# Cross attention: the last context row's values of all 16 heads as two products of 512 columns

## The chip, the cores and the metric

The kernel runs on one core of a Trainium2 chip. The metric is the device time of one execution in microseconds, the median over the runs. The profile is of one execution, with its own time.

## The reference

A block of three layers on x (64 batch items, 32 tokens, 512 channels), each added to its input: cross attention to a context of 257 rows of 256 channels per item, self attention with rotary positions, and a mixture of eight experts of which each token takes two. Only cross attention bears on the change:

```
Q  = (layernorm(x) @ Wq.T)           16 heads of 32
KV = ctx @ Wkv.T                     K and V, 16 heads of 32 each
A  = softmax(Q K^T * 32**-0.5)       over 257 context rows
x  = x + (A V) @ Wo.T
```

All is float32. The kernel makes most large products out of three float32r products each: an operand is split in a high part (rounded to float32r) and a low part (the rest), and high x high, low x high and high x low are added.

## The kernel before

**Tiling.** The 2048 queries are 16 tiles of 128, each four batch items (steps j = 0 to 3, s = 4 i + j) of 32 queries. K and V are never made: `absorb_k` (L353) multiplies the queries with Wk, so that `scores` (L373) works on the context itself, and `gather_z` (L385) makes U, the context summed with the attention weights, which `values` (L397) turns into heads with WvT. The context has 257 rows; 256 make two blocks of 128. The last row has its own way.

**The last row.** In the scores it is a column 256 of zT, filled by POOL (`last_key`, L648). For the values, setup multiplies the last rows of all 64 items with WvT on PE (L234), ACT copies the result to `vl` (L243), and SP stores it in DRAM (L207). For each tile, `last_values` on SP (L305) loads four blocks of 4 rows x 128 columns (512 bytes a row) into `VL` (16 rows x 512, block diagonal: row (m, j) has the values of item j for the four heads of group m in columns m). The weight of the last row is written by DVE to `p_last` (L627), 4 columns a step, at the point where it scales the exponentials; `turn_last` (L369) transposes it on PE into 16 rows in `bank_o`, and `last_rows` on DVE (L586) spreads it with `quad_mask` into `PL`, which is zero except where the row's item is the column's item. `values` then adds, for each of the 16 heads, one product of 16 rows (K) x 32 x 128 columns in full float32 to the two products with WvT:

```
for part in range(KL + 1):          # KL = 2; the third is the last row
    for hh in range(4):             # four column tiles of 32
```

Each float32 product is two records on PE in the profile. The four `hh` are on four column tiles of the array (`tile_position=(0, hh * HD)`).

**Order of the work.** Every engine has its order written out by hand; waits are on semaphores. The loop is by pairs of tiles, the first and last pair apart. PE in step j of tile i: `scores(s)`; at j = 0 `turn_last(i-1)`; `gather_z(s-1)`; at j = 2 `turn_x(i+2)`; `turn_z(s+1)`; `absorb_k`; at j = 0 `values(i-1)`, at j = 1 `project_o(i-1)`, at j = 2 and 3 half of `project_q(i+2)`; `turn_p(s)`. After the loop: `turn_last`, `gather_z`, `values`, `project_o` of the last tile. `scores` writes banks 0 to 3 of `bank_s`, of which 2 and 3 hold the transposed weights of the step before: its third and fourth blocks wait for `v_PT` (L379).

DVE in step j: two `nmax` (L616); at j = 0 `last_rows(i-1)`; at j = 1 `normalise`; reciprocal, `p_last`, scaling of Pr (L628); `qk_lo`, `z_lo`; at j = 0 `statistics` of tile i+2 (L141 to L146; not in the last two tiles) and `ot_lo(i-1)` (L594); `pt_lo` (L580); at j = 1 `add_residual`. ACT: four exp; at j = 0 `u_out`; `qk_hi`; at j = 2 `x_out`; otherwise `u_out`; `qk_out`; `z_hi`; at j = 0 `ot_hi` (L512); `pt_hi`; halves of `q_out`. SP: the four loads of z of a tile, each when its buffer is free, then `last_values`, which waits for `values` of the tile before; in the first tile also the weights of self attention (`ahead`) behind it. POOL: `last_key`, then `split_z` for `gather_z`, and `rstd_of`.

**Before the loop.** `block_constants` (L66) makes the identity and `quad_mask` on POOL in a block of its own, at whose end all engines meet. The setup block loads and transposes the weights; it too ends when all engines, SP's store of `vl` included, have come to its end.

## Time and profile before

| | us |
|---|---|
| median of 3 runs | 1562.9 |
| lowest, highest | 1562.47, 1563.0 |
| the profiled execution, its own time | 1564.86 |
| its span in the trace | 1563.1 |
| PE busy in the span | 1473.5 (94%) |
| DVE, ACT, POOL busy | 1050.5, 828.1, 538.3 |

Busy times are of the whole span; cross attention is its first 726 us, which the loop of tiles fills from about 50 us on. PE is TensorE's products, PEld its weight loads, which overlap them; DVE is VectorE, ACT ScalarE, POOL GpSimd, SP the engine that issues the loads. In a timeline, a row is an instruction or a run of like ones (x4): start and length in us, and in brackets how long the engine had idled before and what released it. Products overlap, so the time one costs is the distance between starts, not its length. PEclk is the granted clock of TensorE as a share of 2.4 GHz.

### The profile page before, as it was taken

To read this page: it belongs to the slowest core of one execution; us is meant where nothing else is said; L and a number is where in the kernel's file an instruction comes from. 1 tells how busy PE (TensorE), PEld (TensorE's weight loads), DVE (VectorE), ACT (ScalarE), POOL (GpSimd) and SP (SyncE) were. 2 spreads that over 40 slices of the span, in tenths; PEclk is the share of its full clock that TensorE was granted. 3 is DMA by queue.
4 is the path that set the end of the run, shared out by engine and by line. 5 is a ranking of instruction groups with operands and counts; after the bars stand their busy time and mean duration, and the time that the engine had idled before them with its cause. 6 is when DMAs were issued, how large, how long until landed. Compare 5 with 4: busy or idle time off the path is not lost. (4 is left out here: it accounts for less than half of the span.)

```text
span 1563.1 us, 40198 instructions
## 1 busy us (share of the span) xinstructions
PE 1473.5 (94%) x15376; PEld 1291.6 (83%) x15376; DVE 1050.5 (67%) x1832; ACT 828.1 (53%) x1542; POOL 538.3 (34%) x821
## 2 busy tenths in 40 slices
PE   5899999999999999997899998679999999999997
PEld 4788888888888888875687777579999999999996
DVE  1566666666666666663557676687878878787884
ACT  3566666666666666653434343154554545555552
POOL 1121222222222222221866777433333332333232
PEclk9999999999999999998999999789999999999999
DMA  8101000000000000000011014147887778787871
GB/s 291 50 22 29 29 23 26 27 20 27 27 27 21 26 27 27 22 15 1 16 37 36 32 41 150 57 150 248 272 273 269 262 245 291 248 265 247 292 240 41
DMA packets 127070, 173.85 MB, mean 111 GB/s; under 512 B 13097, under 2 KB 85737, under 8 KB 126962
## 3 DMA queue, kind: packets, MB, share of 16 engines
q1 hardware_dynamic: 116578, 145.29, 28.5%
q0 software_dynamic: 10384, 27.05, 4.8%
q8 instruction: 76, 1.25, 0.3%
q14 instruction: 32, 0.26, 0.1%
HBM read 157.05 MB, written 18.93 MB: 113 GB/s over the span
## 5 line engine op out<-in xcount | busy, mean ns | idle before, releaser
L1996 DVE TENSOR_TENSOR lo<-raw,hi 128x1024 fp32r<-128x1024 f32 x207 | 246.0, 1219 | 8.7 <-ACT hi L1932 7.4
L52 PE MATMUL mo_bank<-xT_hi,hi 128*128 128x256 f32 x768 | 217.3, 283 | 3.8 <-DVE xT_lo L2005 2.8
L54 PE MATMUL mo_bank<-xT_lo,hi 128*128 128x256 f32 x768 | 216.0, 281 | 0.0
L53 PE MATMUL mo_bank<-xT_hi,lo 128*128 128x256 f32 x768 | 216.0, 281 | 0.0
L1932 ACT CAST hi<-raw 128x1024 fp32r<-128x1024 f32 x207 | 208.3, 1048 | 5.6 <-PEq L842 2.8
L541 ACT ACTIVATE Pr<-xa_s,nmax 128x257 f32<-128x257 f32 x256 | 118.9, 471 | 122.9 <-DVE nmax L616 122.9
L1952 ACT ACTIVATE sl<-mo_bank 128x256 f32<-128x256 f32 x117 | 44.9, 384 | 251.2 <-PE mo_bank L54 251.2
L52 PEld LDWEIGHTS mo_bank<-xT_hi,hi 128*128 128x128 f32 x768 | 145.8, 190 | 10.7 <-issue 6.2
L52 PE MATMUL xa_s<-zT_hi,QK_hi 128*128 128x258 f32 x512 | 150.4, 294 | 2.9 <-DVE zT_lo L570 1.6
L53 PEld LDWEIGHTS mo_bank<-xT_hi,lo 128*128 128x128 f32 x768 | 145.5, 190 | 3.3
L54 PEld LDWEIGHTS mo_bank<-xT_lo,hi 128*128 128x128 f32 x768 | 145.8, 190 | 0.0
L53 PE MATMUL xa_s<-zT_hi,QK_lo 128*128 128x258 f32 x512 | 144.2, 282 | 0.0
L54 PE MATMUL xa_s<-zT_lo,QK_hi 128*128 128x258 f32 x512 | 143.9, 281 | 0.0
L2080 POOL TENSOR_TENSOR e_carrier<-count 128x1 f32<-128x1 f32 x84 | 25.4, 302 | 322.6 <-DMA of_row<-slot_val 114.2
L616 DVE TENSOR_REDUCE nmax<-xa_s 128x2 f32<-128x514 f32 x128 | 88.6, 692 | 47.9 <-PE xa_s L54 47.8
L583 DVE TENSOR_TENSOR PT_lo<-xa_s,PT_hi 128x512 fp32r<-128x512 f32 x128 | 82.3, 684 | 46.5 <-ACT PT_hi L510 46.2
L657 POOL TENSOR_TENSOR xa_carrier<-mhalf 128x1 f32<-128x1 f32 x64 | 12.6, 197 | 289.9 <-DVE QK_lo L575 285.3
L52 PE MATMUL xa_u<-PT_hi,zn_hi 128*128 128x512 f32 x256 | 103.4, 404 | 1.5 <-POOL zn_lo L660 1.5
L53 PE MATMUL xa_u<-PT_hi,zn_lo 128*128 128x512 f32 x256 | 101.5, 397 | 0.0
L54 PE MATMUL xa_u<-PT_lo,zn_hi 128*128 128x512 f32 x256 | 101.3, 396 | 0.0
L52 PE MATMUL mo_bank<-hi,a_hi 128*128 128x512 f32 x234 | 95.9, 410 | 5.2 <-DVE a_lo L2061 5.1
L52 PEld LDWEIGHTS xa_s<-zT_hi,QK_hi 128*128 128x128 f32 x512 | 96.4, 188 | 4.6 <-DVE zT_lo L570 3.0
(290 smaller groups left out, 3921.3 us busy)
## 6 DMA issues: line engine op xcount, KB each, us to landing
raw<-in_L_ffn_W_dram SPq DMA_DIRECT2D x207, 512.0 KB, 5.8
raw<-in_ctx_dram SPq DMA_DIRECT2D x64, 256.0 KB, 2.6
out_dram<-x_res SPq DMA_DIRECT2D x16, 256.0 KB
xs<-xn SPq DMA_DIRECT2D x16, 256.0 KB
x_res<-in_x_dram SPq DMA_DIRECT2D x1, 3840.0 KB, 19.3
raw_o<-in_L_xattn_Wo_dram SPq DMA_DIRECT2D x1, 1024.0 KB, 6.0
raw_q<-in_L_xattn_Wq_dram SPq DMA_DIRECT2D x1, 1024.0 KB, 9.1
VL<-v_last_rows SPq DMA_DIRECT2D x64, 2.0 KB
```

Source lines behind the costliest of these rows:

```text
L52: pe.matmul(out, lh, rh, start=start, stop=False)
L53: pe.matmul(out, ll, rh, start=False, stop=False)
L54: return pe.matmul(out, lh, rl, start=False, stop=stop)
L541: act.activation(Pr[:, m, 0:NK], bank_s[:, m, 0:NK], ACT.Exp, bias=nmax[:, m:m + 1], scale=1.0, accum_out=rsum[:, m:m + 1]).then_inc(a_E, 1)
L583: dve.tensor_tensor(PT_lo[:, c, :], bank_pt[c], PT_hi[:, c, :].bitcast(F32), ALU.subtract).then_inc(v_PT, 1)
L616: dve.tensor_reduce(nmax[:, 2 * h:2 * h + 2], bank_s[:, 2 * h:2 * h + 2, 0:NK], AX_X, ALU.max, negate=True).then_inc(v_mx, 1)
L657: pool.tensor_tensor(carrier[:], mhalf[:], mhalf[:], ALU.add)
L1932: aW.done(act.copy(hi, raw), f"p{c}{q}")
L1952: aM.done(act.activation(sl[:, j % 2, :], bank_hg[j % 2][:, 0:ROWS], ACT.Silu), f"{pos}s{j}")
L1996: vW.done(dve.tensor_tensor(lo, raw, hi.bitcast(F32), ALU.subtract), f"p{c}{q}")
L2080: pool.tensor_tensor(carrier[:], count[:, 0:1], count[:, 0:1], ALU.add).then_inc(carried, 1)
```

## The change

The values of the last row are split in high and low float32r parts in setup (`vl_hi`, `vl_lo`), both stored. `VL` becomes 128 rows x 128 columns: rows (part, head within the group hh, item j, group m), a row's 32 values in columns hh x 32; eight loads of 16 pieces of 128 bytes fill it. `PL` becomes the right side, 128 rows x 512 columns (group, item, query), and `PL_lo` 64 rows x 512. One product VL x PL gives high x high and low x high, since both halves of the rows carry the high weights; VL[0:64] x PL_lo gives high x low. Both go to all of `bank_o` at the start of `values`, and the 32 products with WvT are added to them.

To get the rows, `last_weights` on DVE, behind `pt_lo` of j = 3, splits `p_last` and masks it by head into `p_rows` (128 x 128) and `p_rows_lo` (128 x 64); `turn_last` multiplies these with `key_of` (128 x 32), in two float32r products of 32 columns, and now waits for `v_PR`. `last_rows` makes `PL` and `PL_lo` with two operations. The masks `head_mask`, `row_mask` and `key_of` are made of the identity on DVE in setup; `quad_mask` goes.

```diff
-                pool.affine_select(out=quad_mask[:], in_=quad_mask[:], compare_op=ALU.not_equal, fill=1.0, base=-row,
-                                   pattern=[[-1, 4], [0, 32]], channel_multiplier=1).then_inc(s, 1)
...
-        VL = sb("VL", [LAST_ROWS, C])
+        VL = sb("VL", [P, P], F32R)
+        head_mask = sb("head_mask", [P, HEADS])
+        row_mask = sb("row_mask", [P, BT * NQ])
+        key_of = sb("key_of", [P, HD], F32R)
...
-                    sp.dma_start(vlast_dram, vl[:]).then_inc(vl_put, 16)
+                    sp.dma_start(vlast_dram[0], vl_hi[:].bitcast(F32)).then_inc(vl_put, 16)
+                    sp.wait_ge(lo_done, n_split + 1)
+                    sp.dma_start(vlast_dram[1], vl_lo[:].bitcast(F32)).then_inc(vl_put, 16)
...
-                    act.copy(vl[:], bank_o[0:B, :]).then_inc(hi_done, 1)
+                    act.copy(vl_hi[:], bank_o[0:B, :]).then_inc(hi_done, 1)
...
+                    dve.tensor_reduce(own_key[:], ident[:].rearrange("p (h t) -> p t h", t=HD), AX_X, ALU.add
+                                      ).then_inc(masked, 1)
+                    dve.tensor_reduce(head_mask[:], ident[:].rearrange("p (h t) -> p h t", t=HD), AX_X, ALU.add
+                                      ).then_inc(masked, 1)
+                    for j in range(BT):
+                        dve.tensor_reduce(row_mask[:].rearrange("p (m j) -> p m j", j=BT)[:, :, j],
+                                          ident[:].rearrange("p (b j m) -> p j m b", j=BT, m=NQ)[:, j], AX_X, ALU.add
+                                          ).then_inc(masked, 1)
+                    dve.wait_ge(masked, 2 + BT)
+                    dve.tensor_copy(key_of[:], own_key[:]).then_inc(masked, 1)
+                    dve.wait_ge(hi_done, len(jobs) + 1)
+                    dve.tensor_tensor(vl_lo[:], bank_o[0:B, :], vl_hi[:].bitcast(F32), ALU.subtract).then_inc(lo_done, 1)
+                    dve.wait_ge(lo_done, n_split + 1)
...
-        p_last = sb("p_last", [P, NQ, BT])
-        PL = sb("PL", [LAST_ROWS, NQ, BT, HD])
+        p_last, pl_hi, pl_lo = sb("p_last", [P, BT, NQ]), sb("pl_hi", [P, BT * NQ], F32R), sb("pl_lo", [P, BT * NQ], F32R)
+        p_rows, p_rows_lo = sb("p_rows", [P, 2, HEADS, BT * NQ], F32R), sb("p_rows_lo", [P, HEADS, BT * NQ], F32R)
+        PL, PL_lo = sb("PL", [P, NQ, BT, HD], F32R), sb("PL_lo", [ROWS, NQ, BT, HD], F32R)
...
-                    for m in range(NQ):
-                        sp.dma_start(VL[BT * m:BT * m + BT, m * P:(m + 1) * P],
-                                     vlast_dram[bass.ds(BT * i, BT), m * P:(m + 1) * P]).then_inc(vl_got, 16)
+                    for part in range(2):
+                        for hh in range(HEADS):
+                            w, at = slice(hh * HD, (hh + 1) * HD), part * ROWS + hh * BT * NQ
+                            sp.dma_start(VL[at:at + BT * NQ, w].bitcast(F32),
+                                         vlast_dram[part, bass.ds(BT * i, BT), :].rearrange("j (m w) -> (j m) w", w=P)[:, w]
+                                         ).then_inc(vl_got, 16)
...
-                        sp.wait_ge(vl_put, 16)
+                        sp.wait_ge(vl_put, 32)
...
-                    pe.transpose(bank_o[0:LAST_ROWS, 0:P], p_last[:].rearrange("p m j -> p (m j)"), ident[:]
-                                 ).then_inc(pe_PL, 1)
+                    pe.wait_ge(v_PR, 4 * i + 4)
+                    pe.matmul(bank_o[:, 0:HD], p_rows[:].rearrange("p c h x -> p (c h x)"), key_of[:], start=True, stop=True)
+                    pe.matmul(bank_o[0:ROWS, HD:2 * HD], p_rows_lo[:].rearrange("p h x -> p (h x)"), key_of[:],
+                              start=True, stop=True).then_inc(pe_PL, 1)
...
-                    pe.wait_ge(v_PL, i + 1)
-                    pe.wait_ge(vl_got, 16 * NQ * i + 16 * NQ)
+                    pe.wait_ge(v_PL, 2 * i + 2)
+                    pe.wait_ge(vl_got, 16 * 2 * HEADS * i + 16 * 2 * HEADS)
+                    pe.matmul(bank_o[:], VL[:], PL[:].rearrange("r m j q -> r (m j q)"), start=True, stop=False)
+                    pe.matmul(bank_o[:], VL[0:ROWS, :], PL_lo[:].rearrange("r m j q -> r (m j q)"), start=False, stop=False)
                     for m in range(NQ):
-                        for part in range(KL + 1):
+                        for part in range(KL):
                             for hh in range(4):
                                 h = 4 * m + hh
-                                w = slice(h * HD, (h + 1) * HD)
-                                out = bank_o[hh * HD:(hh + 1) * HD, m * P:(m + 1) * P]
-                                if part < KL:
-                                    mm = pe.matmul(out, WvT[:, part, w], U[:, part, h, :], start=(part == 0), stop=False,
-                                                   tile_position=(0, hh * HD))
-                                else:
-                                    mm = pe.matmul(out, VL[:, w], PL[:, hh].rearrange("r j q -> r (j q)"),
-                                                   start=False, stop=True, tile_position=(0, hh * HD))
+                                mm = pe.matmul(bank_o[hh * HD:(hh + 1) * HD, m * P:(m + 1) * P],
+                                               WvT[:, part, h * HD:(h + 1) * HD], U[:, part, h, :], start=False,
+                                               stop=(m == NQ - 1 and part == KL - 1), tile_position=(0, hh * HD))
...
-                    dve.tensor_tensor(PL[:],
-                                      bank_o[0:LAST_ROWS, 0:P].rearrange("r (h q) -> r h q", q=HD).unsqueeze(2)
-                                      .to_broadcast([LAST_ROWS, NQ, BT, HD]),
-                                      quad_mask[:].unsqueeze(1).to_broadcast([LAST_ROWS, NQ, BT, HD]), ALU.mult
-                                      ).then_inc(v_PL, 1)
+                    for n, (dst, size) in enumerate(((PL, P), (PL_lo, ROWS))):
+                        dve.tensor_tensor(dst[:].rearrange("r m j q -> r (m j) q"),
+                                          bank_o[0:size, n * HD:(n + 1) * HD].unsqueeze(1).to_broadcast([size, NQ * BT, HD]),
+                                          row_mask[0:size, :].unsqueeze(2).to_broadcast([size, NQ * BT, HD]), ALU.mult
+                                          ).then_inc(v_PL, 1)
+
+                def last_weights(i):
+
+                    flat = p_last[:].rearrange("p j m -> p (j m)")
+                    dve.wait_ge(v_N, BT * i + BT)
+                    need(dve, pe_PL, i)
+                    dve.tensor_copy(pl_hi[:], flat).then_inc(v_PR, 1)
+                    dve.wait_ge(v_PR, 4 * i + 1)
+                    dve.tensor_tensor(pl_lo[:], flat, pl_hi[:].bitcast(F32), ALU.subtract).then_inc(v_PR, 1)
+                    heads = [P, 2, HEADS, BT * NQ]
+                    dve.tensor_tensor(p_rows[:], pl_hi[:].bitcast(F32).unsqueeze(1).unsqueeze(1).to_broadcast(heads),
+                                      head_mask[:].unsqueeze(1).unsqueeze(3).to_broadcast(heads), ALU.mult).then_inc(v_PR, 1)
+                    dve.wait_ge(v_PR, 4 * i + 2)
+                    dve.tensor_tensor(p_rows_lo[:], pl_lo[:].bitcast(F32).unsqueeze(1).to_broadcast(heads[:1] + heads[2:]),
+                                      head_mask[:].unsqueeze(2).to_broadcast(heads[:1] + heads[2:]), ALU.mult
...
+                                      ).then_inc(v_PR, 1)
...
-                            need(dve, pe_PL, i)
-                        dve.tensor_tensor(p_last[:, :, j], Pr[:, :, LAST], rinv[:], ALU.mult)
+                            need(dve, v_PR, 4 * i)
+                        dve.tensor_tensor(p_last[:, j, :], Pr[:, :, LAST], rinv[:], ALU.mult)
...
+                        if j == BT - 1:
+                            last_weights(i)
```

## Rows read from the trace of the kernel before

**Rows 1.** Window of one tile: length; busy (count) of PE, PEld, DVE, ACT, POOL; PEclk; DMA.
```profile
340.00:382.00 42.00, 41.91 (x402) 36.12 (x401) 26.84 (x45) 27.61 (x60) 9.83 (x21) 1.00 0.08 24
```

**Rows 2.** Timeline of PE; start us, length us, engine, line, operation, tiles, count
```profile
340.60 0.28 PE L54 MATMUL xa_s<-zT_lo,QK_hi 128*128 128x258 f32 x1
340.72 0.27 PE L370 MATMUL xa_o<-ident,p_last 128*16 128x128 f32 x1
...
341.06 0.39 PE L53 MATMUL xa_u<-PT_hi,zn_lo 128*128 128x512 f32 x1
341.29 0.39 PE L54 MATMUL xa_u<-PT_lo,zn_hi 128*128 128x512 f32 x1
...
344.95 0.65 PE L409 MATMUL xa_o<-U,WvT 128*32 128x128 f32 x16
345.53 0.42 PE L412 MATMUL xa_o<-PL,VL 16*32 16x128 f32 x8
345.88 0.64 PE L409 MATMUL xa_o<-U,WvT 128*32 128x128 f32 x16
...
348.65 1.09 PE L366 MATMUL xa_s<-ident,Pr 128*128 128x128 f32 x8
...
351.03 0.28 PE L52 MATMUL xa_s<-zT_hi,QK_hi 128*128 128x258 f32 x1
...
382.85 0.27 PE L370 MATMUL xa_o<-ident,p_last 128*16 128x128 f32 x1
```

**Rows 3.** Timeline of PE's weight loads at the first change of kind
```profile
345.52 0.15 PEld L412 LDWEIGHTS xa_o<-PL,VL 16*32 16x32 f32 x8 [0.20 <-issue]
```

**Rows 4.** Timeline of DVE around the start of a tile
```profile
341.53 0.67 DVE L588 TENSOR_TENSOR PL<-xa_o,quad_mask 16x512 f32<-16x512 f32 x1
...
342.91 0.17 DVE L627 TENSOR_TENSOR p_last<-Pr,rinv 128x4 f32<-128x4 f32 x1
342.99 1.22 DVE L628 TENSOR_TENSOR Pr<-Pr,rinv 128x1024 f32<-128x1024 f32 x1
...
381.61 0.69 DVE L616 TENSOR_REDUCE nmax<-xa_s 128x2 f32<-128x514 f32 x1
383.05 0.69 DVE L616 TENSOR_REDUCE nmax<-xa_s 128x2 f32<-128x514 f32 x1 [0.75 <-PE xa_s L54]
```

**Rows 5.** Timeline of DVE at the end of step 0
```profile
347.81 0.69 DVE L141 BATCH_NORM_STATS2 st<-x_res 128x6 f32 x1
...
348.75 0.15 DVE L146 TENSOR_SCALAR mv<-mv 128x1 f32<-128x1 f32 x1
349.41 0.69 DVE L596 TENSOR_TENSOR OT_lo<-xa_o,OT_hi 128x512 fp32r<-128x512 f32 x1 [0.51 <-ACT OT_hi L514]
350.02 1.28 DVE L583 TENSOR_TENSOR PT_lo<-xa_s,PT_hi 128x512 fp32r<-128x512 f32 x2
```

**Rows 6.** Timeline of ACT in step 0
```profile
343.81 1.01 ACT L518 COPY U<-xa_u 128x1024 f32<-128x1024 f32 x1 [1.14 <-PE xa_u L54]
...
348.79 0.59 ACT L514 CAST OT_hi<-xa_o 128x512 fp32r<-128x512 f32 x1 [1.62 <-PE xa_o L412]
```

**Rows 7.** Timeline of SP, a tile's loads of VL
```profile
348.92 1.61 SPq L308 DMA_DIRECT2D VL<-v_last_rows  x4
```

**Rows 8.** Timelines of POOL, SP and ACT in the setup
```profile
1.79 1.62 POOL L82 TENSOR_SCALAR_AFFINE_SELECT quad_mask<-quad_mask 16x128 f32<-16x128 f32 x4
...
5.62 0.59 SPq L198 DMA_DIRECT2D raw_zl<-in_ctx_dram  x1
...
22.45 0.58 ACT L243 COPY vl<-xa_o 64x512 f32<-64x512 f32 x1 [1.06 <-PE xa_o L234]
```

**Rows 9.** Timelines of PE and DVE after the loop
```profile
711.62 0.77 PE L52 MATMUL xa_u<-PT_hi,zn_hi 128*128 128x512 f32 x1 [1.50 <-POOL zn_lo L660]
...
711.44 0.67 DVE L588 TENSOR_TENSOR PL<-xa_o,quad_mask 16x512 f32<-16x512 f32 x1
```

**Rows 10.** Window of the gather after the loop
```profile
712.00:715.00 3.00, 3.00 (x8) 2.32 (x8) 0.11 (x1) 0.00 (x0) 0.00 (x0) 0.52 0.00 0
```

33 lines of the change are left out of this document (16 added, 17 removed).

## The prediction

> **What bounds the kernel now.** I read the busy times by slice first, then windows of one query tile each, then the timelines of PE, DVE, ACT and SP over one such tile. Cross attention runs from about 50 to 726 us of the span, and its loop has a period of 42.1 us, a tile of 128 queries (four batch items, steps j = 0 to 3). In a window of 42.00 us PE is busy for 41.91 at full granted clock, DVE for 26.84 and ACT for 27.61 [rows 1]. So PE sets the period: time taken from PE counts, and work given to DVE costs nothing until something PE needs becomes late. The reader should therefore look at spacing between starts on PE, not at durations, and at how far ahead of PE each product of DVE is. Everything behind the stage follows from its end, so I pass a shift on in full.
>
> **The products themselves.** At j = 0 PE runs `values` of the tile before. Its block starts at 344.95 and the next work, `turn_p`, starts at 348.65: 3.70 us [rows 2]. Within it, one group of WvT products takes 345.53 - 344.95 = 0.58 and one group of VL products 345.88 - 345.53 = 0.35, four times each, 0.93 x 4 = 3.70. The 16 records of a WvT group run on four column tiles at once; four records of 128 float32 columns take 2 x 128 / 2.4 GHz = 0.107, so 16 need 0.43 and the 8 of a VL group 0.21. What is left, 0.15 and 0.14, falls where the kind of product changes: the weight loads of the VL group begin only after an idle 0.20 [rows 3]. The block is 2.56 us of columns and eight changes of about 0.14.
>
> After the change: 32 WvT products without interruption, 1.71 us (64 records / 4 x 0.107). Two float32r products of 512 columns at 0.23 each, the spacing of the gather products (341.29 - 341.06 [rows 2]), 0.47 together. The first has a full-width weight load with nothing in front of it: between nothing (after `turn_last`, 341.06 - 340.72 = 0.34 holds a 0.107 transpose and a 0.23 product and no more, the loads being fetched ahead) and the 0.20 of [rows 3]; I take the middle, 0.11. Changes of kind: from the 64-row product to the column tiles and from these to `turn_p`, 0.28, and perhaps one between 128 and 64 rows, of which no row shows a price: 0 to 0.14, I take 0.07. Sum 1.71 + 0.47 + 0.11 + 0.35 = **2.64, against 3.70: 1.06 saved**, bounds 0.9 (0.2 for the start and three full changes) to 1.24 (neither start nor third change).
>
> The trace has idle time wherever K = 128 and K = 16 products meet. The Trainium skill, TensorEngine Tiling (Array Packing), section Key Properties, says that changing the tiling mode drains the engine, and its list of modes has 64 rows as one of its own. By that rule the 128 to 64 row step costs a full change, and the block would be 2.71 instead of 2.64; the trace agrees with the rule for 16 rows and has no case of 64 in this stage.
>
> **turn_last.** Now one transpose, 0.107 us of PE. It becomes two float32r products of 32 columns with 128 and 64 columns of weights. Rows show no such product. Below: two times a sliver, 0.03 each. Above: 0.12 each, the start spacing of a product of 258 columns with full weights (340.72 - 340.60 [rows 2]), which includes its weight load, plus a change of kind on either side (0.28). The nearest row is the 258-column one, because the load and not the columns would decide: 0.24. **Cost 0.13** net, bounds -0.05 to +0.4.
>
> **DVE behind it.** `last_weights` puts four operations between `pt_lo` of j = 3 and `nmax` of the next tile. Sizes: an elementwise operation takes 0.17 for 4 elements and 1.22 for 1024 [rows 4], so 0.165 + 1.03 ns per element: 0.18, 0.18, 0.29 and 0.23 for 16, 16, 128 and 64. A dependent pair starts 0.21 apart, an independent one its length less 0.085 (the two PT_lo take 1.28 [rows 5], 0.68 each). So DVE is held 0.21 + 0.09 + 0.21 + 0.14 = 0.65, and the last result is there after 0.74. In the row, `pt_lo` leaves DVE at 381.61, hence v_PR is complete at 382.35; the scores on PE end at 382.85, where today's transpose starts [rows 2, 4]. `turn_last`, which now waits for v_PR with `gather_z` queued behind it, finds it 0.5 us early: **no wait**. The first `nmax` moves from 381.61 to 382.26 and ends before the second may start, 383.05; exp of heads 0 to 7 comes later and pushes the rest by about 0.25. ACT then has 1.14 us idle before the copy of U, for which it waits on the last product of gather_z [rows 6]: PE fixes that copy, so nothing is passed on. `last_rows` becomes two operations instead of one of 0.67 [rows 4], the second 0.6 more: 342.20 to 342.83, ahead of the exps' new end near 342.9, for which the reciprocal waits. Covered; without that cover it would hold DVE 0.6 us at a place from which PE wants something only at `turn_p`, 4 us after the scaling of Pr at 342.99 [rows 4].
>
> **What is late next.** `scores` of step 1 overwrites bank 2 and must wait for the first PT_lo of step 0. It reaches that product 2.38 us after `turn_p` (351.03 - 348.65 [rows 2]). Today PT_lo starts at 350.02 and ends at 350.71 [rows 5], 0.32 early. With `turn_p` 1.06 - 0.13 = 0.93 earlier, at 347.72, that point is 350.10. ACT can follow: OT_hi starts 0.14 after `turn_p` [rows 6], ends at 348.45. DVE can't: before OT_lo it has z_lo and the statistics of tile i+2, which hang on ACT's copies behind U, not on `values`. They move by +0.13: statistics at 347.94, its last small operation at 348.88, OT_lo at 348.96 instead of 349.41, PT_lo at 349.57, end 350.26, seen at 350.30. So PE waits some 0.2 us, and **the period falls by 351.03 - 350.30 = 0.73, not 0.93.** The second PT_lo (350.92) is just before bank 3 is wanted. Steps 1 to 3 keep their distances. Statistics are left out in the last two tiles: there it is 0.93.
>
> **SP.** `last_values` issues eight loads of 128-byte pieces instead of four; four take 1.61 [rows 7], eight about 3.2. Queued behind is the load of z for step 0 of the next tile, which PE first reads in `turn_z` of j = 3, three steps of 10 us later. 1.6 us of that is nothing. VL itself is read a whole tile later.
>
> **Setup and end.** POOL's four quad_mask selects take 1.62 us, their memset another 0.1, before the first block ends; SP issues its first load at 5.62, when POOL is done [rows 8]. Without them all loads start about 1.7 earlier (0 if another engine were late too, which no row shows). At the end of setup the store of vl waited for ACT's copy (22.45, 0.58); now DVE's subtract (0.69 plus a hop) and a second store follow, and the block can't end before that: +0.73 [rows 8]. The six reductions of ident on DVE lie in its idle time after WoT_lo. Net **-1.0**, bounds -1.7 to +0.8. After the loop, `turn_last` ran while PE waited; gather_z started at 711.62, when PT_lo was done and DVE went on at 711.44 [rows 9] (the row names zn_lo, its other wait; I take PT_lo for the later one). Now last_weights comes first: 711.44 + 0.74 and the two products, so +0.8, of which I take back 0.2, since the granted clock is at 0.52, its lower level of 1.2 GHz, from 712 to 715 after PE had idled [rows 10], and less of the gather falls into that stretch. Then values, -1.06. Net **-0.4**, bounds -1.5 to +1.
>
> **Sum.** Tiles 1 to 13: 13 x 0.73 = 9.5. Tiles 14 and 15: 2 x 0.93 = 1.9. End 0.4, setup 1.0. Together 12.8. The profiled execution took 1564.9 (span 1563.1 and 1.8 around it) and would take 1552.1; the median of the runs, 1562.9, is 2.0 below it, and I forecast **1550.1**.
>
> **Rivals.** (a) DVE is not late: its chain is a little shorter or the statistics slip in earlier, and the whole 0.93 or even 1.1 is kept: 15 x 0.93 to 1.1 + 1.4, or 15 to 18 us, 1547.5 to 1545. For it: DVE is 27 of 42 us busy. Against: the chain above. (b) PE gives more back: the 32-column products cost 0.4, setup gains nothing: 15 x 0.45 + 0 = 7, 1556. For it: a 64-column weight block might be another kind of product. Against: the 16-column transpose in the same place shows no change of kind. (c) Slower: v_PR becomes the wait of PE. Place: after the scores of j = 0, in each tile. Price: what its last result needs beyond 0.74 + 0.5 = 1.24 us, less the 0.93 gained. It decides from 2.2 us on; at 2.6 it is 15 x 0.43 = 6.5 more than before, 1569. For it: broadcast patterns of three free dimensions, for which no SBUF row stands. Against: PL has such a broadcast now, and its 512 elements take 0.67. (d) Nothing moves by over 3 us: the drains are not what fills the 0.14, but a fixed cost per group of products that the 512-column products also pay, and it meets a poor setup: 1561.
>
> **Chances.** Forecast 0.5 (own range 1548 to 1553), (a) 0.2, (b) 0.18, (d) 0.05, (c) 0.07. A measurement of this kernel tells 0.2%, 3.1 us, from no change. (a), the forecast and (b) are all faster: 0.88. Same 0.05, slower 0.07. The range takes in (a) as far as 1545.5 and (b) as far as 1556.5, and leaves out (c) and (d).
>
> **What would show it.** In the changed profile: one block of 64 WvT records without the 0.20 idles, about 1.85 us long; two products of 512 columns with VL before it; the loop's period at 41.4; a new wait of PE on PT_lo in the scores of step 1, about 0.2 each in 13 tiles; no wait of PE on DVE before `turn_last` except the last, near 0.7; SP's first load near 3.9. A period over 41.8 or a wait of PE on p_rows in the loop makes me wrong.

## The result and the profile after

The changed kernel takes 1557.06 us, median of 18 runs (1552.36 to 1562.61), beside 1563.76 (1556.96 to 1567.25, 18 runs) for the kernel before on the same chip: ratio 0.9959, 95% interval 0.9947 to 0.9972. That is faster, since the whole interval lies below 1, by about 6.5 us (0.4%), where I forecast 12.8. The profiled execution took 1560.69, its span 1558.9.

The window of one tile shows the same picture as [rows 1]: PE full, DVE 1.5 us busier.

```profile
338.00:380.00 42.00, 41.82 (x375) 36.77 (x374) 28.33 (x50) 27.66 (x62) 10.17 (x23) 1.00 0.09 25
```

The timeline of PE over the changed part of a tile, to be laid beside [rows 2]:

```profile
337.63 0.18 PE L390 MATMUL xa_o<-key_of,p_rows 128*128 128x32 f32 x1
337.65 0.21 PE L391 MATMUL xa_o<-key_of,p_rows_lo 128*64 128x32 f32 x1
337.71 0.48 PE L52 MATMUL xa_u<-PT_hi,zn_hi 128*128 128x512 f32 x1
...
340.60 0.60 PE L354 MATMUL xa_z<-ident,raw 128*128 128x128 f32 x4
341.13 0.73 PE L377 MATMUL xa_s<-raw,Wk 32*128 32x128 f32 x16
342.04 0.50 PE L423 MATMUL xa_o<-PL,VL 128*128 128x512 f32 x1 [0.18 <-ACT U L536]
342.47 0.49 PE L424 MATMUL xa_o<-PL_lo,VL 64*128 64x512 f32 x1
342.89 1.96 PE L429 MATMUL xa_o<-U,WvT 128*32 128x128 f32 x64
344.78 1.09 PE L385 MATMUL xa_s<-ident,Pr 128*128 128x128 f32 x8
...
347.02 0.28 PE L54 MATMUL xa_s<-zT_lo,QK_hi 128*128 128x258 f32 x1
347.15 0.39 PE L52 MATMUL xa_s<-zT_hi,QK_hi 128*128 128x258 f32 x1
347.37 0.28 PE L53 MATMUL xa_s<-zT_hi,QK_lo 128*128 128x258 f32 x1
```

What to see: `values` is 344.78 - 342.04 = 2.74 us instead of 3.70. Its weight loads are in the timeline of PEld, and those of both large products and of the first column tile each come after an idle time; before, such idle stood at every one of eight changes of kind [rows 3]:

```profile
342.03 0.19 PEld L423 LDWEIGHTS xa_o<-PL,VL 128*128 128x128 f32 x1 [0.37 <-issue]
342.47 0.18 PEld L424 LDWEIGHTS xa_o<-PL_lo,VL 64*128 64x128 f32 x1 [0.25 <-issue]
342.89 0.70 PEld L429 LDWEIGHTS xa_o<-U,WvT 128*32 128x32 f32 x28 [0.24 <-issue]
```

The timeline of DVE shows the new work, ahead of the first `nmax` of the next tile (before, the `nmax` stood there alone [rows 4]):

```profile
336.32 0.17 DVE L617 CAST pl_hi<-p_last 128x16 fp32r<-128x16 f32 x1
336.52 0.18 DVE L619 TENSOR_TENSOR pl_lo<-p_last,pl_hi 128x16 fp32r<-128x16 f32 x1
336.62 0.29 DVE L621 TENSOR_TENSOR p_rows<-pl_hi,head_mask 128x128 fp32r<-128x128 f32 x1
336.82 0.22 DVE L624 TENSOR_TENSOR p_rows_lo<-pl_lo,head_mask 128x64 fp32r<-128x64 f32 x1
336.95 0.69 DVE L650 TENSOR_REDUCE nmax<-xa_s 128x2 f32<-128x514 f32 x1
```

It ends at 337.04, 0.59 before PE wants it at 337.63. `turn_last` starts at 296.1 and, eight tiles later, at 628.2 us: a period of 41.51; before it was 298.6 to 635.6, 42.12. The last add of cross attention starts at 715.0 (725.6 before). So the stage ends 10.6 us earlier, and the span only 4.2: **more than half of the gain of this pair of traces goes away behind the stage.** It has gone by the time of the experts' first cast of x, at 1017.7 (1020.4 before). From last add to first cast are 302.7 us, before 294.8. The timeline of PE shows the largest single piece, in self attention's product for the queries (twelve products of 512 columns):

```profile
957.21 0.47 PE L52 MATMUL sa_bank<-sa_wq_hi,sa_xT_hi 128*128 128x512 f32 x1 [1.01 <-DVE x_res L1252]
961.58 0.58 PE L53 MATMUL sa_bank<-sa_wq_hi,sa_xT_lo 128*128 128x512 f32 x1 [3.90 <-issue]
961.97 0.63 PE L54 MATMUL sa_bank<-sa_wq_lo,sa_xT_hi 128*128 128x512 f32 x1
962.39 0.63 PE L52 MATMUL sa_bank<-sa_wq_hi,sa_xT_hi 128*128 128x512 f32 x1
```

In the trace of before the same product runs through:

```profile
965.95 0.47 PE L52 MATMUL sa_bank<-sa_wq_hi,sa_xT_hi 128*128 128x512 f32 x1 [0.94 <-DVE x_res L1216]
966.26 0.39 PE L53 MATMUL sa_bank<-sa_wq_hi,sa_xT_lo 128*128 128x512 f32 x1
966.50 0.39 PE L54 MATMUL sa_bank<-sa_wq_lo,sa_xT_hi 128*128 128x512 f32 x1
...
968.59 0.39 PE L54 MATMUL sa_bank<-sa_wq_lo,sa_xT_hi 128*128 128x512 f32 x1
```

Between its first and its last product are 2.64 us before and 8.23 after (957.21 to 965.44). 3.90 of the difference is a wait that no semaphore ends ("issue"); most of the rest is the lower granted clock behind it (0.50 from 960 to 964 us): the products follow each other at 0.43 instead of 0.23 us. The windows from 955 to 970 us of the two (before, then after) put the clock at 0.93 and 0.77, and show that the burst of transfers, the experts' first weights, runs over that place in both:

```profile
955.00:970.00 15.00, 13.88 (x310) 11.18 (x309) 9.31 (x30) 3.37 (x6) 8.79 (x11) 0.93 0.95 305
```

```profile
955.00:970.00 15.00, 9.52 (x164) 7.76 (x163) 8.08 (x22) 2.89 (x5) 6.25 (x9) 0.77 0.55 183
```

An engine's own instructions are transfers as well. The page has them as a queue of its own, 1.21 MB in 74 pieces, so 16 KB each:

```profile
q8 instruction: 74, 1.21, 0.3%
```

### The profile page after: what moved, and what is told of

Read it like the earlier page. It is cut to its first block and busy times, and to the rows that moved or that the text cites. A ratio compares the mean times of both kernels' runs of the same rounds, so it can differ in the third digit from the quotient of the medians.

```text
span 1558.9 us, 39528 instructions
## 1 busy us (share of the span) xinstructions
PE 1467.5 (94%) x14912; PEld 1298.3 (83%) x14912; DVE 1068.2 (69%) x1920; ACT 827.7 (53%) x1542; POOL 544.9 (35%) x816
## 3 DMA queue, kind: packets, MB, share of 16 engines
q8 instruction: 74, 1.21, 0.3%
## 5 line engine op out<-in xcount | busy, mean ns | idle before, releaser
L2116 POOL TENSOR_TENSOR e_carrier<-count 128x1 f32<-128x1 f32 x84 | 29.6, 353 | 315.9 <-DMA of_row<-slot_val 106.4
```

The costliest lines, as they stand in the source:

```text
L2116: pool.tensor_tensor(carrier[:], count[:, 0:1], count[:, 0:1], ALU.add).then_inc(carried, 1)
```

## The experiments

Two questions. Where did the gain go behind the stage: is it **Theory C**, that TensorE waits where its unrolled code crosses from one fetched piece to the next, so that the number of instructions ahead of a place decides what it costs; or **K**, clock and chance alone; or later **W**, that TensorE's idle time ahead of self attention sets its clock? And in the stage: which terms make the period 41.51 and not the forecast 41.39?

In what follows the **stretch** is the time from the start of cross attention's last add to the start of the experts' first cast. "Before" beside a time is the kernel before in the runs on the same chip.

**Place of the code, first round.** The changed kernel again, then with 16 and with 32 tiny products ahead of self attention, and the kernel before again. The edit:

```diff
+                for _ in range(32):
+                    pe.matmul(b_lat[0:32, 0:2], ident[:, 0:32], ident[:, 0:2], start=True, stop=True)
                 turn(0)
                 latents(0)
```

> The changed kernel once more, unaltered, for a second trace. Cross attention ended 10.6 us earlier in the first trace, but 6.3 us of that were gone by the end of self attention, 5.6 of them at one place: the queries' product of tile 12 or so in self attention, where PE stood 3.9 us between its first and second product with all data there. Theory C (code): PE waits there for its next block of instructions, whose transfer queues behind the experts' first weight loads; the place is fixed by the count of instructions before it, so the wait of 3 to 5 us is at the same product again. Theory K (clock): what is lost is a matter of where the granted clock falls, another in every execution; then the wait is not at the same product, and the loss between the end of cross attention and 1070 us is spread or absent. Time by both 1552 to 1561.

> The changed kernel with 16 products of 2 columns more at the start of self attention, where PE waits over 4 us for the first normalised tile anyway: every later PE instruction lies some 32 to 64 instructions further on in the code. Theory C: the wait inside the queries' product moves to another place, or shortens, and the time moves by 0 to -4 us against the changed kernel. Theory K: nothing moves but by the spread, the wait of 4 us is where it was if it was there in the unaltered kernel.

> The same with 32 such products, 64 to 128 instructions further on, which is near the number that the change took out of PE's code, counted by blocks of 256. Theory C: the code of self attention is cut about where the kernel before cuts it, the wait of 4 us is gone, and the time is 1553, 4 below the changed kernel. Theory K: no difference to the unaltered one beyond its spread.

> The kernel before once more, unaltered, for a second trace: by theory C without a wait of over 2 us inside a product of self attention again; by theory K such a wait may be anywhere. The place in the head where the clock is low differs from the first trace by both.

Before on that chip took 1567.86. The changed kernel took 1558.22, ratio 0.994 (0.9922 to 0.9957); with 16 tiny products 1556.97, 0.9938 (0.9919 to 0.9957); with 32 it took **1550.42, 0.9888** (0.9849 to 0.9927), though TensorE does more. The kernel before gave 1570.51 in its one run; its expectation was missed, since its second trace has a wait of 2.10 us in self attention, just ahead of the queries' product, where its first trace has none:

```profile
971.87 0.85 PE L921 MATMUL sa_pv<-Kt,Qt 32*32 32x32 f32 x43 [2.10 <-issue]
```

So a cut says where a wait can be, and not that there is one. The waits of 0.9 us or more put down to issue moved with the padding. Timeline of PE, the changed kernel unaltered, then with 32:

```profile
961.23 0.59 PE L53 MATMUL sa_bank<-sa_wq_hi,sa_xT_lo 128*128 128x512 f32 x1 [3.14 <-issue]
...
987.32 0.94 PE L980 MATMUL sa_pv<-Pt,Vt 32*32 32x32 f32 x78 [2.63 <-issue]
```

```profile
977.26 0.38 PE L957 MATMUL sa_bank<-Kt,Qt 32*32 32x32 f32 x12 [1.09 <-issue]
...
981.37 0.35 PE L980 MATMUL sa_pv<-Pt,Vt 32*32 32x32 f32 x14 [2.50 <-issue]
```

The repeat waits at the same product of the same line; with 32 tiny products the queries' product runs through (954.05 to 956.70, 2.65 us). The count of the group behind a wait says where the code is cut, to the product. The second wait stands ahead of a group of 78 in the changed kernel (961.58 and 987.94 in one trace, 961.23 and 987.32 in the other), and of 110 with 16 tiny products, each of which is two records: 78 + 32. With 32 it should be 142, and there is one ahead of 12 and one ahead of 14, and 142 - 14 = 128. In the kernel before it is 123, in both traces:

```profile
989.13 1.24 PE L944 MATMUL sa_pv<-Pt,Vt 32*32 32x32 f32 x123 [1.02 <-issue]
```

So in a run of products alone a cut comes every 128 pairs of weight load and product. A 16 KB piece over 256 instructions would make 64 bytes each (an estimate from these two figures; nothing here shows an instruction's size). Over longer distances it is some 126 recorded pairs: the waits at 930.16, 961.58 and 987.94 in the first trace of the changed kernel are 502 and 505 pairs apart, four pieces each. I take the rest of a piece for other instructions of PE, such as semaphore waits; that was not counted. The changed kernel has fewer products ahead of self attention, and that moved every cut behind it.

**Place of the code, second round.** The law says what padding gives one kernel the other's cuts. I first put 50 tiny products into the kernel before, from a count of source products that overlooked the two records of a float32 product; then 41, worked out from the group counts; and 64 into the changed kernel, one whole piece.

> The kernel before, with 50 tiny products (32 columns of weights, two columns moved, into a bank that is overwritten right after) ahead of self attention's first turn. By the program's own count the changed kernel has 76 products fewer ahead of self attention, so 152 TensorE instructions (a weight load and a product each), and its fetches of instructions are 16 KB each in the trace. If an instruction is 64 bytes (an estimate: nothing in a trace shows it), a piece is 256 of them, and 50 more products put the cuts of the kernel before where the changed kernel has them. Theory C (TensorE waits at a cut in its code whose piece comes late, behind the experts' first weights on the DMA queues): a wait of 3 to 4 us put down to issue appears in or beside the queries' product at about 965 to 975 us, where the kernel before has none, and the stretch from the end of cross attention to the experts' first cast is longer than before's (295 to 301 us) by 2 to 5 us; time 1566 to 1575 us. Theory K (only the clock and the order of the transfers decide how that stretch comes out, the place of the code does not): the padding costs 1.3 us and nothing else, no wait at that place, time within 3 us of the kernel before.

> The kernel before with 41 tiny products ahead of self attention. The runs so far show the law of the cuts: each tiny product stands in the trace as two weight loads and two products, and the count behind the second cut in the experts' transfers went from 78 pairs in the changed kernel to 110 with 16 tiny products (32 pairs more), to 142 (128 and 14) with 32, and is 123 in the kernel before and 95 with 50 tiny products there (100 pairs: 123 less 128 and 100 more). So a piece of code is 128 pairs, and 41 tiny products (82 pairs: 123 + 82 - 128 = 77) put the cuts of the kernel before on the changed kernel's own places. Theory C (the place of the cuts sets the waits): behind the experts' first transfers TensorE waits 3 to 4 us in the queries' product of self attention, at the same product of it as in the changed kernel (the second or the third, high by low half), and 2.5 to 2.8 us ahead of a group of 77 or 78 at about 1000 us; the stretch from the last add of cross attention to the experts' first cast is 301 to 304 us; time 1566 to 1572 us, ratio 1.001 to 1.005. Rival K (clock and chance): no wait over 2 us in the queries' product, the stretch between 295 and 301 us, ratio 1.000 to 1.001.

> The changed kernel with 64 tiny products, 128 pairs, so one whole piece of code more: all cuts fall where they fall with none. They take some 4.3 us, of which some 3 lie in a wait that is there anyway (4.33 us for ScalarE's sa_xn). Theory C: the wait of 3 to 4 us in the queries' product is back, as is the one ahead of a group of 78; the stretch is 301 to 304 us; time 1556 to 1561 us, ratio 0.995 to 0.998. Rival W (the 32 tiny products helped because they fill TensorE's wait ahead of self attention and so keep its clock up, and the cuts do nothing): the gain stays or grows, no wait in the queries' product, stretch 293 to 296, time 1549 to 1553 us, ratio near 0.989.

| kernel | cut ahead of a group of | queries' product, wait in it, us | stretch, us | ratio to before (95%) |
|---|---|---|---|---|
| before (two traces) | 123, 123 | 2.64, none; 3.75, waits 2.10 ahead of it | 294.8, 301.6 | 1 |
| before + 50 | 95 | waits 2.00 ahead of it | 300.5 | 1.0007 (0.9991 to 1.0024) |
| before + 41 | 77 | 7.91, 3.40 | 308.0 | 1.0024 (1.0002 to 1.0045) |
| changed (two traces) | 78, 78 | 8.23, 3.90; 7.14, 3.14 | 302.7, 300.9 | 0.9959, 0.994 |
| changed + 16 | 110 | waits 2.58 ahead of it | 297.3 | 0.9938 (0.9919 to 0.9957) |
| changed + 32 | 14 (and 128) | 2.65, none | 293.7 | 0.9888 (0.9849 to 0.9927) |
| changed + 64 | 78 | 7.11, 2.42 | 302.6 | 0.9956 (0.9941 to 0.9972) |

With 41 tiny products the kernel before waits where it never did, one product further on than the changed kernel, and ahead of a group of 77. Timeline of PE:

```profile
973.30 0.47 PE L52 MATMUL sa_bank<-sa_wq_hi,sa_xT_hi 128*128 128x512 f32 x1 [1.23 <-DVE x_res L1218]
973.61 0.40 PE L53 MATMUL sa_bank<-sa_wq_hi,sa_xT_lo 128*128 128x512 f32 x1
977.41 0.59 PE L54 MATMUL sa_bank<-sa_wq_lo,sa_xT_hi 128*128 128x512 f32 x1 [3.40 <-issue]
977.80 0.63 PE L52 MATMUL sa_bank<-sa_wq_hi,sa_xT_hi 128*128 128x512 f32 x1
```

And with 64 in the changed kernel the wait is back, the group is 78 again, and the gain of the padding is gone, though TensorE is kept busier ahead of self attention than with 32. Part of this is the padding's own time: the first product of self attention comes 7.59 us behind the last add instead of 4.29, so 3.3 of its 302.6 us are that (0.9 of the 308.0 with 41, 1.8 of the 300.5 with 50; with 16 and 32 none). Without them its stretch is 299.3 and its ratio 0.9935, still 5.6 us of stretch above the run with 32. So W falls, and K as the whole of it: the place of the cut decides whether the queries' product is broken, and the law gave that place to the product. The three took 1565.35 (before 1564.14), 1570.21 and 1560.13 us (before 1567.01). The run with 50 missed its forecast twice: the padding took 4.97 us, not 1.3, since it ran at the lower clock, and the cut lay 17 pairs from where I wanted it. The run with 41 met its forecast but for the second wait, 2.36 instead of 2.5 to 2.8, and the stretch, 308.0 instead of 301 to 304; its profiled execution took 1576.63, 6.4 above its median. One thing is not of the cuts: the two traces of the kernel before, with the same cuts, differ by 6.8 us in the stretch, so a single trace must not be read to better than that. The ratios carry the verdict.

**Is it the transfers?** The changed kernel with SyncE starting the experts' first loads a tile of self attention earlier.

```diff
-                    if i == n_early + 3:
+                    if i == n_early + 2:
```

> The changed kernel with the experts' first loads of weights started by SyncE one tile of self attention earlier (at n_early + 2 rather than + 3), so some 16 us earlier: from about 930 rather than 946 us, with the end of the transfers near 947 rather than 963. TensorE's program and its cuts are the same. Theory C (the wait comes of a cut in the code meeting these transfers): at the cut in the queries' product near 960 us, where the changed kernel waits 3.1 to 3.9 us, no wait of 1 us or more is left, and the cut ahead of the group of 23 near 930 us, where it waits 1.08, or another that falls between 930 and 947, waits 2 us or more. The time then depends on what those waits come to: 1552 to 1558 us. Rival N (the wait belongs to that cut, whatever runs on the queues): the wait of 3 to 4 us stays in the queries' product near 960 us, time 1557 to 1559 us.

1555.33 us (before 1567.06), ratio 0.9921 (0.9904 to 0.9937), and a stretch of 296.8 us. The loads started at 935.86 instead of 946.30, so 10 us earlier and not 16, and their transfers still lay over the cut's fetch, near their end. The wait in the queries' product fell, but not under 1 us:

```profile
957.64 0.59 PE L53 MATMUL sa_bank<-sa_wq_hi,sa_xT_lo 128*128 128x512 f32 x1 [2.25 <-issue]
```

Neither expectation is met. Of the six other traces of the changed kernel or its variants with this cut five have 2.94 to 3.90, and the one with 64 tiny products 2.42, so 2.25 is the lowest but not apart from them. And the cut ahead of the group of 78 waits 2.61 us in the changed kernel's trace, when the burst is over. That the transfers lengthen the wait is possible and not shown.

The traces also record every 16 KB transfer of the instructions' queue, with its time. Behind the first 100 us the fourteen traces have 56 waits of 0.9 us or more put down to issue, and 54 of them end 1.25 to 1.57 us after the end of such a transfer (the other two stand at one and the same product with `sa_wo`, in two kernels). That shows more directly than the padding that TensorE waits there for its code. It also tells what a long wait is made of. In the eight traces that wait inside the queries' product the transfer itself took 1.03 to 1.15 us, so it was not slow. What differs is its start: 0.12 us before TensorE fell idle where the wait is 2.25 and 2.42, and 1.25 and 1.36 us after it in the two of 3.90. Why it starts late at some cuts and in time at most others stays open.

**The terms within the stage.** Four edits, two to a kernel, each with a segment of its own in the tile. First:

```diff
-        head_mask = sb("head_mask", [P, HEADS])
+        head_mask = sb("head_mask", [P, 16])[:, 0:HEADS]
...
-                    pe.wait_ge(a_U, BT * i + BT)
                     pe.wait_ge(v_PL, 2 * i + 2)
...
                     pe.matmul(bank_o[:], VL[0:ROWS, :], PL_lo[:].rearrange("r m j q -> r (m j q)"), start=False, stop=False)
+                    pe.wait_ge(a_U, BT * i + BT)
```

> The changed kernel with two edits. First, in the values block the two products of 512 columns go ahead of the wait for U, so that they and the full-width weight load behind them cover that wait. Theory F (the 0.10 us that the block's entry has gained on the kernel before is the wait for ScalarE's copy of U, with the weight load of VL behind it): the wait for U disappears from the entry, the first of the two products starts at 1.25 to 1.30 us after the step before it rather than 1.44, and the loop's period falls by 0.1 to 0.2 us from 41.50. The rival (the entry is set by the keys' block ahead of it and by its change of tile): no change, 41.50. Second, head_mask takes 64 bytes a partition rather than 16, so that what lies behind it in memory is where it was before to 64 bytes. Theory A (the products of the scores take 300 rather than 294 ns since their operands lie 16 bytes off): they fall back to 294, 24 of them from 2.98 to 2.96 us. The rival (clock or order): 300 ns as in the changed kernel.

Second (the statistics move behind `pt_lo` on DVE):

```diff
-        PL, PL_lo = sb("PL", [P, NQ, BT, HD], F32R), sb("PL_lo", [ROWS, NQ, BT, HD], F32R)
+        PL, PL_lo = sb("PL", [P, NQ, BT, HD], F32R), sb("PL_lo", [P, NQ, BT, HD], F32R)
...
-                    pe.matmul(bank_o[:], VL[0:ROWS, :], PL_lo[:].rearrange("r m j q -> r (m j q)"), start=False, stop=False)
+                    pe.matmul(bank_o[:], VL[:], PL_lo[:].rearrange("r m j q -> r (m j q)"), start=False, stop=False)
...
-                        dve.tensor_tensor(dst[:].rearrange("r m j q -> r (m j) q"),
+                        dve.tensor_tensor(dst[0:size].rearrange("r m j q -> r (m j) q"),
...
+                dve.memset(PL_lo[ROWS:P].rearrange("r m j q -> r (m j q)").bitcast(F32), 0.0)
...
-                        if j == 0 and more:
-                            statistics(dve, i + 2)
                         if j == 0 and not first:
                             ot_lo(i - 1)
                         pt_lo(s)
+                        if j == 0 and more:
+                            statistics(dve, i + 2)
```

> The changed kernel with two edits. First, the low half's product has all 128 rows (the lower 64 of its right operand are set to zero once, its left operand is the whole of VL), so that there is no change from 128 to 64 rows. Theory R (a change of the number of rows costs what a change of the width of the tile costs, 0.14 to 0.2 us, and the second product pays it): the block from its first product to its last falls from 2.74 to 2.45 to 2.60 us. The rival (the 0.42 us of a product of 512 columns is the reading of float32r operands from the previous result, or the change at the first of the 32-column tiles, whatever the rows): 2.74 stays. Second, the statistics of the tile after next, 0.8 us of VectorE work, go behind the low half of the turned weights in the first step of a tile. Theory P (TensorE waits 0.11 us for it at the third group of the scores in each tile): the wait goes, the groups follow each other at 0.12 us, and the period falls by 0.1; the rival (the wait is for ScalarE's high half): it stays. Together, period 41.50 to 41.1 to 41.3 by both theories.

Distances between starts on PE, in us, in the tile that begins at the second `turn_last` of the loop's window, and the period over eight tiles:

| | changed | first pair | second pair | all four |
|---|---|---|---|---|
| keys' block (L377) to VL product | 0.91 | 0.66 | 0.90 | 0.66 |
| two VL products | 0.85 | 0.84 | 0.66 | 0.66 |
| 24 products of scores, step 1 | 3.08 | 3.31 | 2.97 | 2.96 |
| the same, steps 2, 3, 0 | 2.99, 2.99, 2.97 | 2.96, 2.98, 2.96 | 2.99, 3.00, 2.97 | 2.96, 2.97, 2.95 |
| WoT products | 2.91 | 2.87 | 2.90 | 2.87 |
| period | 41.51 | 41.40 | 41.22 | 40.85 |

The segments vary by 0.01 to 0.02 us from tile to tile. Theory F holds: the products cover the wait for U and the weight load, 0.25 us. But the first pair shows what it is worth alone. The scores of step 1 grow from 3.08 to 3.31, since PE comes 0.25 earlier to a product that waits for PT_lo, and PT_lo hangs on DVE, which has not moved. Timeline of PE in that kernel:

```profile
346.15 0.28 PE L54 MATMUL xa_s<-zT_lo,QK_hi 128*128 128x258 f32 x1
346.53 0.39 PE L52 MATMUL xa_s<-zT_hi,QK_hi 128*128 128x258 f32 x1
```

0.38 from start to start where 0.12 is the rule. The wait took the place of the one removed, and the period fell by no more than the second edit brings: 0.03 + 0.01 + 0.01 + 0.04 = 0.09 of 0.11. That edit only moves what lies behind a 16-byte tile by 48 bytes, and the scores' and WoT products get shorter, as Theory A has it. But this edit always ran together with the one at the entry: the place in memory is the likely cause, as these products stand elsewhere in the tile, but it is not shown alone. In the second pair Theory R holds too: with 128 rows in both products they follow at 0.34 and 0.32 instead of 0.43 and 0.42, 0.19 saved, and with the statistics behind PT_lo its wait is gone (3.08 to 2.97):

```profile
337.77 0.49 PE L423 MATMUL xa_o<-PL,VL 128*128 128x512 f32 x1 [0.18 <-ACT U L536]
338.11 0.40 PE L424 MATMUL xa_o<-PL_lo,VL 128*128 128x512 f32 x1
338.43 1.95 PE L429 MATMUL xa_o<-U,WvT 128*32 128x128 f32 x64
```

These two kernels ran once each, at 1552.94 and 1551.72 (before 1564.14).

**All four together**, with 32 tiny products and with none.

> The four edits of the two runs before this one together, and the 32 tiny products ahead of self attention. By the theories: the period of the loop 41.50 less 0.1 to 0.2 (wait for U) less 0.15 to 0.3 (rows) less 0.1 (statistics), some 0.4 us in each of 15 tiles or 6 us, and the wait at the cut in the code (3.9 us in the changed kernel) moved out of the stretch with the weights' transfers only if the cuts fall as in the run with 32 tiny products, which they do by Theory C, since no product is added or taken away. Time 1542 to 1547 us. By the rivals (the edits move nothing, the padding alone works): 1550 us as with the padding alone. If the low time of that run was chance and not the cuts: 1550 to 1555.

> The four edits together without the tiny products. Theory C and the terms read from the four traces (entry 0.25, block 0.19, wait for the low half 0.11, places in memory 0.12 us in a tile, period 40.85 us as with the padding): the wait of 3 to 4 us in the queries' product is back, and the time is 1546 to 1550 us, ratio 0.987 to 0.990, so 7 to 10 us above the run with the padding. Rivals W and K (the padding did not work by the cuts): W as Theory C, since the clock falls without the padding, but with no wait in the queries' product; K 1539 to 1543 us.

With them **1539.52 us, ratio 0.983** (0.9809 to 0.9851; before 1564.14), below the 1542 to 1547 that I expected: the fastest kernel of this study, 24.6 us below the kernel before by the medians. Without them 1547.18, ratio 0.9871 (0.9847 to 0.9896; before 1567.01). The period of 40.85 is what the terms sum to: 0.25 (entry) + 0.19 (rows) + 0.11 (wait for PT_lo) + 0.12 (places in memory, second pair against all four) = 0.67, and 41.51 - 40.85 = 0.66; now that the wait for PT_lo is gone, the 0.25 is kept. Without padding, the wait is back at the same product, as Theory C had it:

```profile
950.30 0.59 PE L53 MATMUL sa_bank<-sa_wq_hi,sa_xT_lo 128*128 128x512 f32 x1 [3.24 <-issue]
```

The four edits add and remove no product, so the cuts of this kernel are the changed kernel's. The two kernels with the four edits differ by 0.0041, some 6 us, by the padding alone, beside 7.8 us for the changed kernel (1558.22 to 1550.42); in neither case do the times of the two kernels' runs overlap.

## Why the prediction was right and wrong

**The direction and the mechanism within the stage were right; the size was not: 12.8 us forecast, some 6.5 measured, and 1557.06 is 0.6 above the range.**

**The step that failed** is "Everything behind the stage follows from its end, so I pass a shift on in full." The stage ended 10.6 us earlier in the first pair of traces and 11.0 in the second (716.3 against 727.3), but the medians fell by 6.7 us on one chip and 9.6 on the other. In the first pair 302.7 - 294.8 = 7.9 us of stretch came on top, 5.6 of it in one product (8.23 - 2.64). The second pair shows that this pair is an extreme: there the stretches are 300.9 and 301.6, nothing is given back, and the profiled executions lie 12.0 us apart. It is the pair in which the kernel before has the wait of 2.10 us. So by the medians some 1 to 4 us are lost behind the stage.

I had counted products removed for their time and not for their number. That the place of the cuts matters is shown on the changed kernel: with cuts that miss the queries' product it gives 0.9888 instead of 0.994. What the change's own shift of the cuts cost is less firm. The kernel before with the changed kernel's cuts takes 1.0024, 3.8 us of 1567, of which 0.9 is the padding's own time; the interval, less that, reaches from nothing to 6 us. At equal cuts (the changed kernel with 64 tiny products against the kernel before with 41, on one chip) the change gives 0.9956 / 1.0024 = 0.993, which is 10.7 us, or some 13 without the paddings' own time. Either agrees, within some 4 us of noise, with the 10.6 and 11.0 by which the stage ends earlier. I had no rival for this, and the trace of before had the signs: a queue of instruction transfers on its page, and waits put down to issue.

**The smaller miss is in the stage.** From the first `turn_last` to the last gather I forecast 13 x 0.73 + 2 x 0.93 - 0.8 = 10.6 us, and it is 8.7 in both pairs, most of it by the period's 0.62 in place of 0.73 (13 x 0.11 = 1.4).

Point by point, within the stage:

- **The products themselves.** 2.74 us against my 2.64, and my sum held 0.11 for the start, which in the trace comes in front of the 2.74 (next point). Two float32r products 0.85 with the full third change of kind, 64 WvT records 1.89. The step from 128 to 64 rows, for which I took 0.07, costs the 0.2 of a full change (0.19 came back with 128 rows). The Trainium skill, TensorEngine Tiling (Array Packing), section Key Properties, has the tiling mode's change drain the engine, and the page's list of modes has 64 rows; these rows agree.
- **The start of the block.** I took 0.11 for the weight load and no wait in front of it. The entry cost 0.91 - 0.66 = 0.25 in all, 0.10 more than the 0.81 of before: the wait for ACT's U was there before, hidden behind the load of a small tile, and the full-width load now comes after it. I had written that PE fixes that copy, so nothing is passed on; the copy was not later, but what stands behind the wait was.
- **turn_last.** From the last product of the scores through to the gather I expected 0.13 more than before; it is 0.06, within the bounds. Rival (b), which had 0.4 here, had the right total for the wrong reason.
- **DVE behind it.** Held 336.32 to 336.95, 0.63 (forecast 0.65); v_PR complete 0.59 ahead of PE (0.5). No wait in the loop, so rival (c) never came near.
- **What is late next.** The wait for PT_lo is where I put it, at 0.11 rather than 0.2: PE also arrives later than I had it, by the 0.10 longer block and 0.10 at the entry, less the 0.07 by which `turn_last` is shorter. The period fell by 0.62, not 0.73. The places in memory are a term that I did not have: steps 2 and 3 of the scores take 2.99 instead of the 2.97 and 2.98 of before, some 0.05 in a tile; the WoT products took 2.91 before too.
- **SP.** Eight loads take 3.85 us instead of my 3.2; nothing waits for them.

```profile
345.04 3.85 SPq L326 DMA_DIRECT2D VL<-v_last_rows  x8
```

- **Setup.** SP's first load is at 3.74 (5.62 before), as forecast. But the first `turn_last` is at 88.6, against 88.0 before: in the window from 21 to 50 us the clock is 0.76 instead of 0.82 (the second trace of the changed kernel has 0.76 there too and its first `turn_last` at 87.5, so the clock there is not the whole of it). Over all traces it is at 88.0, 88.3, 90.6 and 88.0 in the kernels built on the one before and from 86.2 to 89.1, 87.5 on average, in the ten built on the changed one: 1.2 less than the 88.7 of the others, about the 1.0 that I forecast, but the traces scatter by more than that.

```profile
3.74 0.59 SPq L198 DMA_DIRECT2D raw_zl<-in_ctx_dram  x1
```

- **The end.** The last `turn_last` waits for v_PR as I wrote, from 702.96 on, when the last of the four results is under way. In this trace the end came out better than forecast, by luck: from the start of the gather to the last add are 11.5 us instead of 14.0, since the gather ran at full clock, where before it ran at the lower of the two levels, 1.2 GHz [rows 10]. In the second pair the clock is 0.50 and 0.53 there, and the same distance is 14.0 against 15.4: 1.4 less, near the forecast for `values`. Timeline of PE and window of that gather:

```profile
703.32 0.25 PE L390 MATMUL xa_o<-key_of,p_rows 128*128 128x32 f32 x1 [2.28 <-DVE p_rows_lo L624]
```

```profile
703.50:706.50 3.00, 3.00 (x14) 2.13 (x13) 1.28 (x2) 0.00 (x0) 0.00 (x0) 1.00 0.00 0
```

The sum for this pair of traces, by starts: setup +0.6; from the first `turn_last` to the last gather 623.6 before (88.0 to 711.62) and 614.9 after (88.6 to 703.48), -8.7; from that gather to the last add 14.0 and 11.5, -2.5, of which 0.96 is `values`; together -10.6. Then the stretch gives 7.9 back, and 1.5 is regained behind it, for a span 4.2 shorter.

Of the 6.3 us between forecast and result the stage holds about 2 (12.8 against 10.6 and 11.0). The other 4 went behind it. The cuts hold some 3 of them by the runs with padding (3.8 less 0.9), with an interval that begins at nothing; the rest is within the scatter of the runs.

## What to carry to other kernels

Before passing a gain on to the end, look behind the stage for waits put down to issue, and ask whether the change alters the number of instructions of an unrolled engine program: here every product removed moved all later cuts of TensorE's code, and 32 tiny products in a wait that is there anyway brought about as much again as the change itself (0.994 to 0.9888 on one chip). And take one saving at a time to the next wait: 0.25 us at the entry was worth nothing until the statistics were out of PT_lo's way. A kernel with padding chosen for one program must be measured again after each edit.

## What the runs showed of the hardware that was not expected

- TensorE's unrolled code is fetched in pieces of 128 pairs of weight load and product (fewer where other instructions stand between); a cut can cost 1 to 4 us of waiting, which ends 1.25 to 1.57 us after the 16 KB transfer has landed, and when the wait is long, the lower clock behind it: the products of the queries then follow each other at 0.43 instead of 0.23 us. Most cuts show no wait of 0.9 us.
- Giving the second of two 512-column products 128 rows like the first, instead of 64, saved 0.19 us over the two, about what a change of the column tile costs [rows 3].
- Moving the operands by 48 bytes shortened 24 products of 258 columns by 0.02 to 0.03 us and 12 of 512 columns by 0.04. Which tile's place does it, and the edit by itself, was not tried.
- The same tiny products took 2.16 us for 64 records in one kernel and 4.97 us for 100 in another, 0.034 and 0.050 each, by the clock they met (1.00 and 0.57).
